# The expert stage's loaded operands moved by 64 bytes in every partition: from 64 to 128 modulo 256

## What is computed

```python
h = layernorm(x) * (1 + ca) + sa
# mixing: four 256 -> 512 products, a scan over time, a 512 -> 256 product
K = sigmoid(xn @ W_K); u, g_in, g_out = split(xn @ W_ugg)
...
x = x + ga * (outputs * g_out @ W_out + h)
h = layernorm(x) * (1 + cb) + sb
# experts
gate_scores = softmax(h @ Wg + bg)            # top 2 of 8, renormalised
for e in range(8):
    y = gelu(h @ W1[e] + b1[e]) @ W2[e] + b2[e]   # 256 -> 1024 -> 256
    output = output + y * combine_w[..., e:e + 1]
x = x + gb * output
```

## The kernel before, in words

| buffer | role in a matmul | before: starts at, modulo 256 | with the change |
|---|---|---|---|
| SH0, SL0 (W1 part) | loaded | 106816, 123456: 64, 64 | 106880, 123520: 128, 128 |
| SH0, SL0 (W2 part) | streamed | 115200, 131840: 0, 0 | the same |
| SH1, SL1 (W1 part) | loaded | 148544, 165184: 64, 64 | 148608, 165248: 128, 128 |
| SH1, SL1 (W2 part) | streamed | 156928, 173568: 0, 0 | the same |
| fh, fl | streamed | 142336, 144384: 0, 0 | the same |
| hl, hh | loaded | 181824, 190016: 64, 64 | 181888, 190080: 128, 128 |
| xin | transposed | 140096: 64 | 140160: 128 |
| ysb, ytmp | none | 198208, 200256: 64, 64 | 198272, 200320: 128, 128 |
| fr | streamed (half tiles) | 202304: 64 | 202368: 128 |
| wraw, h2all | loaded (half tiles) | 50304, 16512: 128, 128 | the same |
| WH, WL / xh, xl | loaded / streamed (mixing) | 0 / 0 | the same |
| wog0, wog1 / og | streamed / loaded (projection) | 64, 0 / 0 | the same |

## Time and profile before

### The profile page before, as it was taken

How to read it: one execution, slowest core, us unless ns; L and a number is a source line. 1 busy time by engine, 2 the same in 40 slices (tenths; PEclk the granted TensorE clock), 3 DMA queues, 4 the chain that set the end, 5 groups by cost and what they waited for, 6 DMA issues and landing times.

```text
span 722.1 us, 16046 instructions
## 1 busy us (share of the span) xinstructions
PE 678.8 (94%) x4798; PEld 621.9 (86%) x4798; DVE 506.7 (70%) x1751; ACT 417.1 (58%) x1068; POOL 399.5 (55%) x318
## 2 busy tenths in 40 slices
PE   5799999999999999998989999999999999999992
PEld 2578888788888887888979999999999999999992
DVE  5869789998989797585844557557875576576551
ACT  4555655556465554565455646757666566566460
POOL 2165536787767468257664437336656356374443
PEclk9899999999999999899999999999999999999997
DMA  8370011302202423245444353566654545543443
GB/s 303 108 251 26 34 60 52 112 31 89 69 22 90 139 83 107 37 117 141 113 82 67 70 131 66 123 146 179 134 124 75 149 109 125 140 70 68 70 75 45
DMA packets 50604, 72.77 MB, mean 101 GB/s; under 512 B 5969, under 2 KB 42397, under 8 KB 50529
## 3 DMA queue, kind: packets, MB, share of 16 engines
q0 software_dynamic: 16480, 27.28, 20.3%
q1 hardware_dynamic: 34048, 44.60, 20.0%
HBM read 48.85 MB, written 23.01 MB: 100 GB/s over the span
## 4 chain that ended last, share of the span: by engine, by line
PE 79%; DVE 7%; issue 4%; DMA 4%; ACT 2%; POOL 2%; another core or an unknown queue 0%; DVEq 0%; SPq 0%; POOLq 0%; ACTq 0%
PE yb L1152 23%; PE mm L1027 21%; PE mm L1136 18%; PE yb L1052 7%; PE tp L1127 2%; PE yb L1136 2%; PE tp L1136 2%; DMA gbr<-mod_rows,xm 1%; DMA out_x<-ysb,tokb 1%; PE mm L1143 1%; PE tp L1042 1%; DVE ytmp L1607 1%; DVE ysb L1615 1%; DMA h2all<-in_L_wmod 1%; PE tp L1063 1%
## 5 line engine op out<-in xcount | busy, mean ns | idle before, releaser
L695 POOL DMA_INDIRECT out_x<-ysb,tokb x68 | 110.9, 1631 | 172.5 <-DVE ysb L1615 129.9
L951 ACT ACTIVATE hh<-mm,vT 128x256 fp32r<-128x256 f32 (+1 forms) x232 | 110.1, 475 | 136.3 <-PE mm L1136 120.5
L1152 PE MATMUL yb<-SH,hh 128*128 128x256 f32 x544 | 157.2, 289 | 2.7 <-DVE hl L1586 1.8
L1152 PE MATMUL yb<-SL,hh 128*128 128x256 f32 x544 | 152.6, 280 | 0.9 <-issue 0.9
L1152 PE MATMUL yb<-SH,hl 128*128 128x256 f32 x544 | 152.7, 281 | 0.6 <-issue 0.4
L1586 DVE TENSOR_TENSOR hl<-mm,hh 128x256 fp32r<-128x256 f32 (+1 forms) x232 | 93.2, 407 | 73.8 <-ACT mm L952 52.1
L1136 PE MATMUL mm<-fh,SH 128*128 128x256 f32 x416 | 119.8, 288 | 8.0 <-DVE hl L1586 3.3
L1136 PE MATMUL mm<-fl,SH 128*128 128x256 f32 x416 | 117.2, 282 | 0.0
L1136 PE MATMUL mm<-fh,SL 128*128 128x256 f32 x416 | 117.2, 282 | 0.0
L1027 PE MATMUL mm<-xh,WH 128*128 128x512 f32 x256 | 107.3, 419 | 1.7 <-DVE xl L1342 1.5
L1152 PEld LDWEIGHTS yb<-SH,hh 128*128 128x128 f32 x544 | 103.2, 190 | 4.0 <-DVE hl L1586 3.2
(11 more groups left out here) (263 smaller groups left out, 1416.6 us busy)
## 6 DMA issues: line engine op xcount, KB each, us to landing
xin<-disp_x SPq DMA_DIRECT2D x74, 132.0 KB
wraw<-in_L_ffn_W SPq DMA_DIRECT2D x8, 1024.0 KB
h2all<-in_L_ffn_W SPq DMA_DIRECT2D x8, 1024.0 KB
xb<-in_L_attn_x SPq DMA_DIRECT2D x8, 512.0 KB, 7.1
out_x<-x2b SPq DMA_DIRECT2D x8, 512.0 KB
mb<-mod_rows SPq DMA_DIRECT2D x3, 768.0 KB, 6.2
wraw<-in_L_attn_W_ugg SPq DMA_DIRECT2D x1, 1536.0 KB, 11.5
gbr<-mod_rows,xm POOLq DMA_INDIRECT x74
```

The lines of the kernel that those rows point to most:

```text
L695: e.indirect_dma_start(out=out_rows, out_offset=bass.IndirectOffsetOnAxis(ap=tokb[:, j:j + 1], axis=0), in_=ysb[:, j, :], in_offset=None, ...
L951: e.activation(hh[:, f, c_], u, ACT.Gelu_apprx_tanh, bias=bias)
L1152: i = e.matmul(yb[0][:, j * D:(j + 1) * D], a[:, f, j * 128:(j + 1) * 128], b[:, f, :], start=(f == 0 and j == 0 and t == 0), stop=(f == N ...
```

## The change

The loaded operands of the expert stage start 64 bytes later in each partition. A gap of 64 bytes is put before `SH0`, the gap behind `xin` shrinks by as much, the gap before `SH1` grows by as much, and the offset of W2 within the split buffers shrinks by as much. No instruction is added, removed or moved.

```diff
--- before.py
+++ after.py
@@ -26,7 +26,7 @@
 CAP = TOK
 MAGIC = 0x5F3759DF
 LINE = 16
-W2_AT = 2048 + 3 * LINE
+W2_AT = 2048 + 2 * LINE
 
 NE0, NE = 5, 8
 SPARE = E * CAP + E * 256
@@ -151,10 +151,11 @@
             xh[0] = sb(gone, "xh0", [128, 2, T], F32R)
             xl[0] = sb(gone, "xl0", [128, 2, T], F32R)
 
+        sb(ctx, "gap3", [128, LINE])
         SH[0] = sb(ctx, "SH0", [128, 4096 + 4 * LINE], F32R)
         SL[0] = sb(ctx, "SL0", [128, 4096 + 4 * LINE], F32R)
         xin = sb(ctx, "xin", [128, 2, DW])
-        sb(ctx, "gap1", [128, 2 * LINE])
+        sb(ctx, "gap1", [128, LINE])
         fh = sb(ctx, "fh", [128, 2, TE], F32R)
         fl = sb(ctx, "fl", [128, 2, TE], F32R)
         gbr = sb(ctx, "gbr", [128, 2, D])
@@ -176,7 +177,7 @@
             cy = sb(mixing, "cy", [128, 4])
             lgT = sb(mixing, "lgT", [128, 128])
 
-        sb(ctx, "gap2", [128, LINE])
+        sb(ctx, "gap2", [128, 2 * LINE])
         SH[1] = sb(ctx, "SH1", [128, 4096 + 4 * LINE], F32R)
         SL[1] = sb(ctx, "SL1", [128, 4096 + 4 * LINE], F32R)
         hl = sb(ctx, "hl", [128, NF, TE], F32R)
```

## The result

The changed kernel takes 731.18 us (median of 6 runs, 729.67 to 732.94) against 725.32 us of the kernel before (6 runs, 721.87 to 727.54): the ratio is 1.0066, interval 1.0035 to 1.0098. The ratios and their 95% intervals are estimated from the single runs; they are not the quotients of the medians (here 1.0081). I had forecast 725.0 us and no change. The median lies inside the stated range and within 1%, but the interval excludes 1: the kernel became slower, by 5.9 us between the medians, and by a mechanism (one longer step in every tile) to which I had given 0.28 in two rivals.

The account below looks back on a forecast made before the run. TensorE's stream and weight loads, both full in the experts' loop, were taken as the bound. Four terms of 0 us on the profiled 724.07 us, with the runs' median 1.05 us above, gave 725.0 us; range 718.5 to 741.

Parts of the forecast that it names:

- two rivals: Experts' loop: all tiles long (0.14) and the worse lock (0.14), both with a longer step in every tile.
- What bounds the kernel: Experts' loop of whole tiles, 410 to 708 us: TensorE busy 296.31 of 298 us, its weight loads 294.33.
- the mixture: Experts' tiles at steps of 113.3 or 117.9 ns, seven long pieces of 17, mean 115.2 ns per matmul.
- (a): Loaded operands of the experts' 3168 256-column matmuls (L1136, L1152): step unchanged by the new distance, 0 us.
- the short step: Experts' layer 1 matmuls 113.3 ns from start to start, claimed the same at distances 0 and 64, 0.443 ns a column.
- all tiles long: Experts' loop: at the new distance every tile settles on 117.9 ns, +8.6 us, 734 us; chance 0.14.
- The change doesn't do what it says: Experts' tiles: alignment has no say, steps drawn anew by each break, 725 us; chance inside the forecast's 0.54.
- The worse lock: Experts' loop: stream and load collide once more per matmul, 121.5 ns gives 745 us, 125 ns 756; chance 0.14.
- b: Half tiles: fr moves from 64 to 128, 128 matmuls of L1143, at most 0.6 us either way, taken as 0.
- c: DMAs into xin and out of ysb: some tenths of a us more stay covered, 0 us.
- d: DVE and ScalarE writes of the moved hl and hh: 1% on them moves less than 0.1 us, taken as 0.
- The sign that I named for long steps: TensorE's groups of loads: a mean of 192 ns for one of three marks a tile of long steps.

Follow-up runs that it names:

- The pair without the addition: Kernel before and changed kernel, each with the indirect DMA that adds the experts' results into the output left out: 719.07 and 726.77 us.

## Why the prediction was wrong, by its steps

**What bounds the kernel: right.** The loop is full on both sides of TensorE and every ns of the step counts there; the two steps of before and their share came back in each profile of that layout.

**The step that failed: "I take the mixture as unchanged, 0 us" in (a).** I argued that the short step is the same at distance 0 and 64, since 512-column matmuls at distance 0 and 256-column ones at 64 both take 0.443 ns a column. But distance 0 was seen only where the load has slack. At full load it gives 120.0 ns. I had written down that such rows "can't exclude a cost that only a full load shows", and then took their side. In the place of the 0 us the runs put one settled step in every tile, so that the mean of the settled intervals goes from 115.2 ns to 118.6 at distance 128: +3.4 ns for each of 3168 matmuls, up to 10.8 us. That the median fell inside the stated range is owed to the range, which was wide enough to hold "all tiles long", and not to the forecast of no change.

**Distances and steps at full load**, from the runs: 0: 120.0 ns; 32: 118.3; 48 and 80: some 118 to 120, in layer 1 at times 114; 64: 113.3 or 117.9; 128: 118.3 to 118.8, in one run 120.0 in four tiles; 192: 117.9.

**The rivals.** "All tiles long" was the nearest: one step for all tiles, chosen by the distance. It was mis-sized in the step (118.6 in place of 117.9 ns; +10.8 us in place of +8.6) and in what reaches the clock. "The change doesn't do what it says" is refuted by the runs with one side moved each. The Trainium skill ("TensorE: Matmul & The Clock Gate", Part 2, step by step) has the two read ports independent, so that loading the next weights takes nothing from the running matmul. The traces disagree with what follows from that: at full load the load's start relative to the stream changes the matmul's step by 6.7 ns (120.0 against 113.3). Whether the two meet at the ports or elsewhere they don't show. The worse lock at 121.5 ns or more was seen at no distance tried.

**The size.** Between the two profiled executions the spans grew by 8.1 us, and the starts of TensorE's matmuls from 276 us on account for it. The settled intervals (under 122.5 ns) take 353.7 us in place of 343.2, so +10.4 before rounding. The other 190 or so intervals of the same matmuls, those with a wait, at half clock or behind a break, take 50.8 in place of 52.5; my product with all 3168 charged the longer step to these too. Transposes, half tiles and the rest take 35.6 in place of 36.3. The pair without the addition repeats it: +10.9, -1.6 and -1.3 us. The granted clock is 0.979 before and 0.981 after, so (1 - 0.979) x 722.1 = 15.2 us of clock were lost before and 13.9 after, most of the difference where the early tiles are (0.95 against 0.96 from 276 to 410 us). In the pair without the addition the clock went the other way (0.984 to 0.981), so it is not what gives the time back each time; what does stays open. Between medians the cost was 5.9, 7.3 (loaded operands alone), 6.8 (streamed side moved), 4.5 (the change again on another chip) and 7.7 us (no addition). The share of short tiles in the kernel before wasn't profiled on each of those chips, and how much of this spread is that share stays open.

**The parts at nothing** (b, c, d): the run with xin, ysb and fr put back kept the whole cost (ratio 1.0095), so these carry none of it that shows. The sign that I named for long steps, a load of 192 ns in three, holds for the long step of before but not for the new one, whose loads all take 188 or 189 ns; the chain's pieces were the sign that worked.

## What to carry to other kernels

Where TensorE's loads and its stream are both full, the time between starts depended, in this kernel, on where the loaded operand starts relative to the streamed one, modulo 256 bytes; here 64 was the only distance of seven with a short step in whole tiles, and missing it costs 0.6 to 1.1%. A row from a stage in which the loads have slack says nothing about it. Read the pieces of the chain in order of time per matmul, not mean durations, and profile twice before taking a mixture as fixed.

## What the runs showed that I had not expected

The same instructions settle on a step and keep it for a whole tile; a break of four transposes redraws it. Where xin starts may shift the draw: four short of twenty with xin at 128 and the operands as before, against ten of seventeen and eleven of sixteen with xin at 64. That is one profile on another chip, and with both sides moved xin also lay at 128 and seventeen of eighteen were short, so xin alone doesn't decide it.

Chips differ by more than the change: beside these runs the kernel before took a median of 710.2 and 710.86 us on two chips and 725 to 729 on others. The changed kernel's first and second profile, 730.2 and 712.6 us of span, have the same step (118.6 and 118.7 ns) and differ almost wholly in the intervals that aren't settled, 50.8 against 27.4 us. A profile on the first of them (xin alone at 128) has no half clock between 276 and 410 us and 1121 matmuls in these 134 us, where the earlier trace rows has 968 at a clock of 0.95:

```profile
276.00:410.00 134.00, 131.19 (x1121) 129.01 (x1119) 89.35 (x346) 84.79 (x216) 79.77 (x68) 1.00 0.51 112
```

What the early tiles wait for on the other chips wasn't tested.
